# Values a chunk after their unit, denominators a chunk later, K and V in pairs, and another order of the first batch, in an attention layer between two routed feed-forward layers

## What is computed

```python
x = x + 0.5 * ffn(layernorm(x))        # 768 of 1024 tokens, chosen by a router score, go through gelu(x @ w_block)
x = x + attention(layernorm(x))        # 16 heads of 32, causal
x = x + 0.5 * ffn(layernorm(x))
# attention, per batch
q_lat  = einsum('bthd,hdl->bthl', (h @ Wq.T).reshape(b, t, 16, 32), q_to_latent)
logits = einsum('bthl,bsl->bhts', q_lat, h @ Wk_down.T) / sqrt(64)      # latents of 64
attn   = softmax(where(causal, logits, -1e30))
ctx    = einsum('bhts,bsl->bhtl', attn, h @ Wv_down.T)
out    = einsum('bhtl,hld->bthd', ctx, v_up).reshape(b, t, 512) @ Wout.T
```

## Time and profile before

| | us |
|---|---|
| median of 3 runs | 2327.71 (2326.27 to 2329.19) |
| the profiled execution | 2326.99 |
| its span | 2325.1 |
| TensorE busy in it | 2153.9 (93%) |
| VectorE busy | 1760.4 (76%) |
| ScalarE busy | 1101.7 (47%) |
| GpSimd busy | 488.9 (21%) |

### The profile page before, as it was taken

One profiled execution on the slowest core, in us unless ns is written; L12 is line 12 of the kernel. 1 busy time (PEld: TensorE's weight loads), 2 busy tenths in 40 slices (PEclk: granted clock), 3 DMA queues, 4 the chain that ended last, 5 costly groups with the idle time before them and its releaser, 6 DMA issues.

```text
span 2325.1 us, 52505 instructions
## 1 busy us (share of the span) xinstructions
PE 2153.9 (93%) x21256; PEld 1314.2 (57%) x21256; DVE 1760.4 (76%) x5017; ACT 1101.7 (47%) x1942; POOL 488.9 (21%) x574
## 2 busy tenths in 40 slices
PE   5589999999999999999999999999999999999997
PEld 4454477545775456744667446764466544775446
DVE  5668857887678876798677886788857888578747
ACT  2335643456425554255543565435643456435562
POOL 2201212114112231023210232111221113121132
PEclk8789999999999999999999999999999999999999
DMA  4300021210212103021021210211111120212000
GB/s 140 145 1 32 9 73 40 104 42 2 91 55 74 38 14 98 37 74 38 20 91 38 74 39 24 87 44 69 39 58 52 55 93 3 73 37 74 2 2 37
DMA packets 71934, 123.16 MB, mean 53 GB/s; under 512 B 2832, under 2 KB 33040, under 8 KB 67600
## 3 DMA queue, kind: packets, MB, share of 16 engines
q1 hardware_dynamic: 71696, 119.81, 14.8%
HBM read 81.53 MB, written 37.75 MB: 51 GB/s over the span
## 4 chain that ended last, share of the span: by engine, by line
PE 78%; DVE 12%; ACT 5%; issue 4%; POOL 1%; DMA 0%; DVEq 0%; POOLq 0%; SPq 0%; ACTq 0%
PE psum L860 29%; PE psum L873 18%; PE psum L994 11%; PE psum L1001 10%; PE psum L876 5%; DVE part L1143 3%; ACT pr L840 2%; PE psum L887 2%; DVE psum L1145 2%; PE psum L912 2%; DVE junk L1095 1%; DVE junk L1093 1%; DVE qk L1132 1%; PE psum L918 1%; ACT nt_h L746 1%
## 5 line engine op out<-in xcount | busy, mean ns | idle before, releaser
L840 ACT ACTIVATE pr<-psum 128x512 f32<-128x512 f32 x1152 | 617.8, 597 | 525.2 <-PE psum L876 525.0
L873 PE MATMUL psum<-qk,qk 32*128 32x512 f32 (+3 forms) x4608 | 515.3, 370 | 60.6 <-DVE part L1143 22.8
L1145 DVE CUSTOM_DVE_ANT_0 psum<-psum,mask_b 128x512 f32<-128x512 f32 (+3 forms) x1024 | 472.8, 521 | 105.5 <-PE psum L887 103.5
L873 PEld LDWEIGHTS psum<-qk,qk 32*128 32x128 f32 x4608 | 318.5, 186 | 384.0 <-ACT pr L840 337.5
L887 PE MATMUL psum<-qk,qk 32*128 32x512 f32 (+3 forms) x4608 | 511.7, 370 | 20.6 <-DVE part L1143 19.1
L1143 DVE TENSOR_REDUCE part<-psum 128x1 f32<-128x512 f32 x512 | 325.0, 681 | 54.7 <-PE psum L887 52.2
L887 PEld LDWEIGHTS psum<-qk,qk 32*128 32x128 f32 x4608 | 311.0, 186 | 43.0 <-DVE part L1143 22.9
L994 PE MATMUL psum<-pr,v_sb 128*32 128x512 f32 (+3 forms) x3072 | 314.6, 504 | 2.3 <-ACT ht L746 1.6
L1001 PE MATMUL psum<-pr,ones 128*32 128x512 f32 (+3 forms) x3072 | 306.4, 494 | 0.0
L738 POOL TENSOR_SCALAR_AFFINE_SELECT pr<-pr 128x512 f32<-128x512 f32 x256 | 162.0, 654 | 558.4 <-ACT pr L840 556.3
L860 PE MATMUL psum<-wb_h,nt_h 128*128 128x512 f32 x512 | 208.0, 406 | 10.9 <-DVE wb_l L1042 7.0
(11 more groups left out here) (116 smaller groups left out, 3368.0 us busy)
## 6 DMA issues: line engine op xcount, KB each, us to landing
nt_raw<-x_turned_dram SPq DMA_DIRECT2D x16, 1024.0 KB, 6.1
x<-x_dram SPq DMA_DIRECT2D x16, 1024.0 KB, 7.1
spill_x<-x SPq DMA_DIRECT2D x16, 1024.0 KB, 4.7
x<-spill_x SPq DMA_DIRECT2D x16, 1024.0 KB, 6.9
out_dram<-x SPq DMA_DIRECT2D x14, 1024.0 KB, 4.9
w_h<-scratch_o SPq DMA_DIRECT2D x28, 256.0 KB, 3.0
w_l<-scratch_o SPq DMA_DIRECT2D x28, 256.0 KB, 3.3
w_h<-scratch_q SPq DMA_DIRECT2D x6, 1024.0 KB, 4.9
```

Source lines behind the costliest of these rows:

```text
L840: nc.scalar.activation(pr_of(b, g, u)[:, 2 * p + place, :], bank(e, place), ACT.Exp, scale=SCALE).then_inc(exp_ready, 1)
L873: eng.matmul(o, (k_h, k_h, k_l)[t][own, P * j:P * (j + 1)], (q_h, q_l, q_h)[t][own, queries], start=(t == 0 and at == 0), stop=False, skip ...
L1145: m = nc.vector.tensor_tensor_reduce(scores, scores, mask_b[:, BANK - w:BANK], 1.0, FAR, ALU.add, ALU.max, top_of)
```

## The change

`values(n)` (PV and AC) of a unit now stands behind chunk b of the next unit, where it stood behind chunk a of the unit after that. `sums(n)` (DEN and HT) now stands behind chunk a two units later, where it stood behind chunk b. So the two fillings change places and the values come one chunk earlier. At the end of a group what fills the last chunk b is now the values of u7. In group 3 they stand ahead of `F` of tile 1.

Each K is followed by a V in the table, and their six matmuls are issued in turns, K, V, K, V, K, V. TensorE waits for both banks before the first.

In the first batch the statistics of both halves come ahead of the centring and the split of the block weight (`WC`, `WS 0`), all eight router dots come before the first `F`, both broadcasts (`SC`) behind the second `F`, and the splits of the latent and K/V weights before all `RT`. The split of Wq stands inside the second norm's scales, and the split of Wout, now in a buffer of its own, behind the first `Q`. In `closing()` the last `SC` stands behind the layer's tile 5 instead of ahead of it.

```diff
--- before.py
+++ after.py
@@ -123,37 +123,36 @@
     def opening():
 
 
-        out = [("WC", 0)] + sum([raw(0, i) for i in range(TC)], []) + [("WS", 0)]
+        out = sum([raw(0, i) for i in range(TC)], [])
         for c in range(NC):
             for i in range(TC * c, TC * (c + 1)):
                 out += stats(0, 0, i)
             out += scales(0, 0, c)
-        out += sum([raw(0, i) for i in range(TC, NT)], [])
-        for i in range(TC):
+        out += [("WC", 0), ("WS", 0)] + sum([raw(0, i) for i in range(TC, NT)], [])
+        for i in range(NT):
             out += dot(0, 0, i)
-        out += layer(0, 0, 0) + layer(0, 0, 1)
-        for i in range(TC, NT):
-            out += dot(0, 0, i)
-        out += [("SC", 0, 0, 0)] + layer(0, 0, 2) + [("SC", 0, 0, 1)] + [("RT", 0, 0, i) for i in range(3)] + [("WS", 1)]
-        out += [("RT", 0, 0, i) for i in range(3, 6)] + layer(0, 0, 3) + [("WS", 2)] + [("RT", 0, 0, 6), ("RT", 0, 0, 7)]
-        out += [("RF", 0, 0)] + [("GX", 0, 0, i) for i in range(NT)] + [("WS", 3)] + layer(0, 0, 4) + layer(0, 0, 5)
-        out += layer(0, 0, 6) + layer(0, 0, 7)
-        out += summed(0, 0) + summed(0, 1) + summed(0, 2) + summed(0, 3) + scales(1, 0, 0) + [("WS", 4)]
+        out += layer(0, 0, 0) + layer(0, 0, 1) + [("SC", 0, 0, 0), ("SC", 0, 0, 1), ("WS", 1), ("WS", 2)]
+        out += [("RT", 0, 0, i) for i in range(NT)]
+        for i in range(2, NT):
+            out += layer(0, 0, i)
+        out += [("RF", 0, 0)] + [("GX", 0, 0, i) for i in range(NT)]
+        out += summed(0, 0) + summed(0, 1) + summed(0, 2) + summed(0, 3)
+        out += [("VA", 1, 0, 0), ("RS", 1, 0, 0), ("WS", 3), ("NM", 1, 0, 0)]
         out += [("NO", 1, 0, 0), ("NO", 1, 0, 1)]
         after = [summed(0, 4), summed(0, 5), summed(0, 6), summed(0, 7) + scales(1, 0, 1)]
         for i in range(TC):
             out += [("T", 1, 0, i)] + ([("NO", 1, 0, i + 2)] if i + 2 < TC else []) + after[i]
-        out += [("LAT", 0, 0), ("XS", 0, 0), ("NO", 1, 0, 4), ("NO", 1, 0, 5), ("K", 0, 0, 0)]
-        out += [("Q", 0, 0, 0), ("T", 1, 0, 4), ("NO", 1, 0, 6), ("T", 1, 0, 5), ("NO", 1, 0, 7)]
+        out += [("LAT", 0, 0), ("XS", 0, 0), ("NO", 1, 0, 4), ("NO", 1, 0, 5), ("K", 0, 0, 0), ("V", 0, 0)]
+        out += [("Q", 0, 0, 0), ("WS", 4), ("T", 1, 0, 4), ("NO", 1, 0, 6), ("T", 1, 0, 5), ("NO", 1, 0, 7)]
         out += [("Q", 0, 1, 0), ("T", 1, 0, 6), ("T", 1, 0, 7)] + maxima(0, 0, 7) + [("LAT", 0, 1), ("XS", 0, 1)]
-        out += [("XL", 1, 0), ("XL", 1, 1), ("K", 0, 0, 1), ("Q", 0, 0, 1)]
-        beside = [[("Q", 0, 1, 1)], [("K", 0, 1, 0), ("K", 0, 1, 1)], [("V", 0, 0), ("V", 0, 1)], [("Q", 0, 2, 0)],
-                  [("Q", 0, 2, 1)], [("Q", 0, 3, 0)], [("Q", 0, 3, 1)], [("V", 0, 2), ("V", 0, 3), ("V", 0, 4)]]
+        out += [("XL", 1, 0), ("XL", 1, 1), ("K", 0, 0, 1), ("V", 0, 1), ("Q", 0, 0, 1)]
+        beside = [[("Q", 0, 1, 1)], [("K", 0, 1, 0), ("V", 0, 2)], [("K", 0, 1, 1), ("V", 0, 3)], [("Q", 0, 2, 0)],
+                  [("Q", 0, 2, 1)], [("Q", 0, 3, 0)], [("Q", 0, 3, 1)], [("K", 0, 2, 0), ("V", 0, 4), ("K", 0, 2, 1), ("V", 0, 5)]]
         for u, rest in zip((0, 1, 2, 3, 4, 5, 6, 8), beside):
             out += maxima(0, 0, u) + rest + sum([gathered(0, 0, c) for c in range(NC) if LAST[c] == u], [])
             out += turned(0, 0, 1) if u == 8 else []
-        out += [("V", 0, 5), ("V", 0, 6), ("V", 0, 7), ("K", 0, 2, 0), ("K", 0, 2, 1)] + turned(0, 0, 0)
-        return out + [("K", 0, 3, 0), ("K", 0, 3, 1)]
+        out += [("K", 0, 3, 0), ("V", 0, 6)] + turned(0, 0, 0)
+        return out + [("K", 0, 3, 1), ("V", 0, 7)]
...
-        out += [("Q", b, 0, 0), ("Q", b, 1, 0), ("K", b, 0, 0), ("T", 1, b, 4), ("NO", 1, b, 6)]
+        out += [("Q", b, 0, 0), ("Q", b, 1, 0), ("K", b, 0, 0), ("V", b, 0), ("T", 1, b, 4), ("NO", 1, b, 6)]
...
-        out += [("Q", b, 0, 1)] + loads[0] + keys[1] + [("V", b, 0)] + splits[0] + [("V", b, 1)] + splits[1]
+        out += [("Q", b, 0, 1)] + loads[0] + keys[1] + [("V", b, 1)] + splits[0] + splits[1]
...
-            groups[g].append(combined(n, 0) + (then(n - 3, "HR") if n >= 3 else []) + (values(n - 2) if n >= 2 else []))
+            groups[g].append(combined(n, 0) + (then(n - 3, "HR") if n >= 3 else []) + (sums(n - 2) if n >= 2 else []))
             groups[g].append(combined(n, 1) + (then(n - 3, "HE") if n >= 3 else []) + mask(n) + [("MC", *e) for e in closes(n)]
-                             + ([("XT", *e) for e in closes(n - 1)] if n else []) + (sums(n - 2) if n >= 2 else []))
+                             + ([("XT", *e) for e in closes(n - 1)] if n else []) + (values(n - 1) if n >= 1 else []))
         last = len(units) - 1
-        return groups, [then(last - 2, "HR") + then(last - 2, "HE") + values(last - 1), sums(last - 1), values(last),
+        return groups, [then(last - 2, "HR") + then(last - 2, "HE") + sums(last - 1), values(last), [],
                         sums(last) + then(last, "HR") + then(last, "HE")]
...
-        out += dot(1, b, 3) + layer(1, b, 4) + turn(3) + [("SC", 1, b, 0)] + layer(1, b, 5)
+        out += dot(1, b, 3) + layer(1, b, 4) + turn(3) + layer(1, b, 5) + [("SC", 1, b, 0)]
...
+    for e, after in zip(sched, sched[1:]):
+        if e[0] == "K":
+            assert after[0] == "V"
+            beside[e] = after
...
-            raws = [(raw_b, w_block), (raw_lat, w_lat), (raw_kv, None), (raw_o, w_out), (raw_q, w_q)]
+            raws = [(raw_b, w_block), (raw_lat, w_lat), (raw_kv, None), (raw_q, w_q), (raw_o, w_out)]
...
                         sp.wait_ge(split, 8)
-                        eng.dma_start(scratch_o[0], w2_h[:].bitcast(F32)).then_inc(scr_out, 16)
-                        eng.dma_start(scratch_o[1], w2_l[:].bitcast(F32)).then_inc(scr_out, 16)
-                        sp.wait_ge(split, 10)
                         eng.dma_start(scratch_q[0], w2_h[:].bitcast(F32)).then_inc(scr_out, 16)
                         eng.dma_start(scratch_q[1], w2_l[:].bitcast(F32)).then_inc(scr_out, 16)
+                        sp.wait_ge(split, 10)
+                        eng.dma_start(scratch_o[0], wo_h[:].bitcast(F32)).then_inc(scr_out, 16)
+                        eng.dma_start(scratch_o[1], wo_l[:].bitcast(F32)).then_inc(scr_out, 16)
                         sp.wait_ge(scr_out, 64)
...
-                    if n == 4:
-                        act.wait_ge(scr_out, 32)
...
+                    if b == 0 and g >= 2:
+
+                        act.wait_ge(scr_out, 64)
...
-                    pe.wait_ge(split, 10)
+                    pe.wait_ge(split, 8)
...
-                    passes(bank(e), (wkv_h, wkv_l), (lat_h, lat_l), 1, lambda w, n: w[0:L, P * g:P * (g + 1)],
-                           lambda t, n: t[0:L, c * BANK:(c + 1) * BANK]).then_inc(k_done, 1)
-                elif k == "V":
-                    b, i = e[1:]
+                    v = beside[e]
+                    i = v[2]
                     pe.wait_ge(latl_ready, nth["LAT", b, i // TC])
-                    passes(bank(e), (lat_h, lat_l), (wkv_h, wkv_l), 1, lambda t, n: t[L:P, P * i:P * (i + 1)],
-                           lambda w, n: w[L:P, :]).then_inc(v_done, 1)
+                    for user in before[v]:
+                        pe.wait_ge(*freed(*user))
+                    for t, (w, l) in enumerate([(wkv_h, lat_h), (wkv_h, lat_l), (wkv_l, lat_h)]):
+                        m = eng.matmul(bank(e), w[0:L, P * g:P * (g + 1)], l[0:L, c * BANK:(c + 1) * BANK],
+                                       start=(t == 0), stop=(t == 2))
+                        if t == 2:
+                            m.then_inc(k_done, 1)
+                        m = eng.matmul(bank(v), l[L:P, P * i:P * (i + 1)], w[L:P, :], start=(t == 0), stop=(t == 2))
+                        if t == 2:
+                            m.then_inc(v_done, 1)
```

14 lines of the change are left out of this document (9 added, 5 removed).

## The result

The changed kernel takes 2344.16 us (median of 4 runs, 2340.82 to 2348.22) where the kernel before takes 2326.99: ratio 1.0073, interval 1.0057 to 1.0090. It is **slower by 17 us**, outside the range of the prediction and on the other side of the forecast. The profiled execution has a span of 2338.9, 13.8 above the 2325.1 of before.

What follows compares the result with a forecast made beforehand. TensorE, busy 93% of the span, was taken to bound the kernel. Gains of about 30 us against losses of about 26 summed to -4.6, giving 2322.4, or 2323 with 0.7 for the median; range 2308 to 2339.

Steps and rivals of the forecast that it cites:

- 4: Turns of a group: covering TensorE's 0.63 us wait saves 0.55 at 16 turns and 0.5 at 8, -12.8 us.
- 5: End of group 3: values of u7 wait 2.4 us for their mask behind eight GX on POOL, seven times, +16.8 us.
- 6: Step into the latents: one filling less between the last transpositions doubles the 0.41 us wait for VectorE, +2.8 us.
- 7: Granted clock: may drop to half behind the mask wait, less a gain at batch starts, +6.3 us.
- step 1: Opening of batch 0: earlier statistics and ranking, K and V in turns, earlier attention start, -4.8 us.
- 3: First units of a batch: values of u0 fill TensorE's 1.83 us wait for VectorE's maxima, -6.3 us.
- 2: K and V in later batches: issued as pairs, one triple less, 0.7 us in each of 7 batches, -4.9 us.
- 8: End of the last batch: AC of u6 issued a chunk earlier removes a 1.64 us wait for ScalarE, -1.7 us.
- D: K and V: matmuls start strictly in program order, so pairs save two more steps each, -22.5 us, 2301; chance 0.04.
- rival E: Turns of a group: the 0.63 us wait only moves to short fillings in u7 and u8, 2336; chance 0.12.
- rival C: Behind the mask wait: clock drops for 6.6 us at 0.56, 3.3 us lost by each of 7, 2338; chance 0.17.

Runs made afterwards that it cites:

- e1: Changed kernel with the values of u7 in group 3 put back among the next batch's first transpositions: 2307.1 us, ratio 0.9913 to the kernel before.
- e8: Kernel before with the changed opening alone, K and V as before, no swap, old closing: 2325.0 us, ratio 0.9989.
- e4: Kernel before with one part alone, each K issued in turns with a V: 2322.7 us, ratio 0.9985.
- e9: Kernel before with only the values of u0 of batches' first group moved early, behind chunk b of u1: 2338.1 us, ratio 1.0042.
- e6: e1 with the last tile of u5's filling (128 columns) moved to u6: 2301.4 us, ratio 0.9893 to the kernel before.
- e10: Kernel before with 128 columns of u5's fillings moved to u6's, values and denominators where they were: 2319.6 us, ratio 0.9966.
- e2: Changed kernel with the eight GX on POOL behind the mask of u7 in group 3, values still early: 2309.2 us, ratio 0.9920 to the kernel before.
- e7: e1 with the values of u0 of each batch put back late, behind chunk a of u2: 2316.1 us, ratio 0.9954 to the kernel before.
- e5: Kernel before with the swap of values and denominators alone, values of u7 of group 3 staying among the transpositions: 2314.6 us, ratio 0.9952.

## Why the prediction was wrong, step by step

The forecast's sum was -4.6 us; it came out at +13.9 by the profiles (2338.93 against 2325.06) and +17 by the medians. The step that failed by most is 4: the turns of a group were to save 12.8 us and saved some 2, because the waits stayed with the short fillings of u6. With it the size of what follows the wait for the mask was too small (steps 5, 6 and 7: 28.0 forecast, 34.9 measured), and the opening gave 2.1 instead of 4.8.

The table sets the forecast beside the traces, stretch by stretch, as the difference to the kernel before. Its bounds in each batch are the starts of the 1st, 21st, 91st and 121st of the 144 exps (the last two are in the middle of groups 2 and 3), then the start of the next batch's latents and the end of its last K or V. From the 21st exp to the 121st, the kernel after and e1 have done one filling more than the kernel before by the same exp. An estimate of 0.88 us for it (the shortest time of eight such matmuls at full clock) is counted as a gain in the first units and taken off again behind the 121st exp, so the second, fifth and last rows are estimates to that extent.

| stretch | forecast | after | e1 |
|---|---|---|---|
| to the first exp of batch 0 (step 1) | -4.8 | -2.1 | -2.0 |
| first five units of each batch (3, and its clock) | -8.4 | -9.4 | -9.5 |
| 16 turns into groups 1 and 2 (4) | -8.8 | 0.0 | -0.5 |
| 8 turns into group 3 (4) | -4.0 | -2.2 | -2.2 |
| rest of group 3 to the next batch's first latents, 7 times (5, 6, 7) | +28.0 | +34.9 | -0.4 |
| from there to the last K or V, 7 times (2) | -4.9 | -4.7 | -4.5 |
| from there to the next attention | 0 | -1.6 | +1.3 |
| last batch, rest of group 3 to the end (8) | -1.7 | -0.9 | -0.8 |
| sum | -4.6 | +13.9 | -18.6 |

**1. Opening (-4.8 forecast, 2.4 of it K and V).** The way was right as far as the latents. TensorE's first F starts at 27.16 (27.4 said), the ranking at 41.74 (41.6 said), the first latents 3.65 us sooner. The size was not. The first exp of batch 0 is 2.1 us sooner, where the forecast said some 5 for the first scores, and without K and V (e8) it is 0.85.

**2. K and V (-4.9).** The stretch gained 4.7 us in the kernel after, and e4 measured -4.5 in all. Right, and so was the verdict on D.

**3. First units (-6.3, and -2.1 for the clock).** The step said that the values leave the path because they fill the wait. They fill it, but another opens: 1.57 us, ended by VectorE's maxima, since VectorE is the bound there, as the step itself noted. TensorE's idle time in this stretch is 4.7 us *more* than before over the eight batches. What falls is its busy time, with 41 us less at half clock. So the total came out near the forecast (-9.4 against -8.4) by luck: the filled wait, put at 6.3, gave nothing, and the clock, put at 2.1, gave all of it. Alone, the move costs 10 us (e9).

**4. Turns (-12.8).** I covered the wait of 0.63 and put 0.55 down as saved. By the waits, each turn has 0.14 us less (1.04 to 0.90), 3.4 for 24 turns. By the exps it is less still: the lead over the kernel before is 2.75 us ahead of the first turn of batch 1 and 2.6 in the middle of group 1. The 16 turns into groups 1 and 2 gain nothing together, the 8 into group 3 0.27 each. That is the outcome of rival E, to which I gave 0.12. The counterargument was wrong: that ScalarE's exp ends the wait doesn't save it, since a short filling in another place meets the same way over ScalarE to a free bank. E's own reason, that VectorE's maxima set the pace, isn't what the trace shows either; the 0.49 is ended by ScalarE. e6 and e10 show the part of the short fillings from the other side.

**5. Mask (+16.8).** Measured 19.6, seven waits of 2.8 us in the mean, in the range given. The mechanism and its place were right. e1 and e2 show it twice: by moving the values back, and by moving GX on POOL.

**6. Latents (+2.8).** Measured +6.3, 0.9 a batch. The term was mis-sized: I took the wait to double, but VectorE's chain has little slack there, and 0.9 of the 1.33 us of missing filling comes back as a wait.

**7. Clock (+6.3).** Behind the mask 30.7 us were at half clock, where I had 7 x 3.4 x 0.7 = 16.7. In the fifth stretch of the table TensorE is busy 11.5 us longer in the kernel after than in e1, with the same matmuls; that is the cost, where I had 8.4. Three of the six drops lasted 6.8 us, rival C's case, to which I had given 0.17. The answer to C, that TensorE had been busy for 100 us there, misread the rows: its last wait, 0.63 us, was 32 us earlier (546.23 in the kernel before), and in the kernel after 33 us. At the starts of the batches 41 of 44 us of half clock went (seven places of 3.4 to 6.8 us before, one of 3.4 after), for which I had taken off 2.1 us of time.

**8. End (-1.7).** The wait of 1.64 is gone. The kernel after is 15.55 us behind at the last exp and 13.9 at the end. That is -1.7, of which 0.46 is the filling of u6 that the kernel after had done by then. So the stretch gave somewhat less than the size given.

So E came in nearly whole and C by half: 10.6 us less from the turns, 6.9 more behind the mask and at the latents, 2.7 less from the opening. Each of the two rivals stood in the list by itself, and the range ended at 2339 because I left out the case of both. The profiled execution of the kernel after is the fastest of its four; the 3 us between it and the median aren't explained.

How the gain of step 3 divides between levels of clock and waits isn't settled by an experiment of its own: e7 and e9 change the waits as well as the clock, and which of the waits drop the clock was not the same from batch to batch. That the clock is what gives the gain there rests on the busy and idle times of one profile each.

## What to carry to other kernels

When work is moved ahead in a queue, look up who must release it and what is queued ahead of that release on *its* engine: here one mask of 0.6 us behind eight unrelated operations turned a gain of 20 us into a loss of 17, and changing the order on that lightly used engine was enough to get it back. A wait that disappears from its place is not saved until the trace shows that the same releaser does not end a new one a few steps later; count all the waits of the cycle, not the one that is covered. Where an engine's work is moved from one stage to another, ask whether it covered a wait in the stage that it leaves (here the values of u7 did, ahead of the latents: 6.3 us).

## What was not expected of the hardware

- Waits of 2.7 us in TensorE's queue, after 30 us of unbroken work and more, were followed by half clock in six of seven cases, for 3.4 or 6.8 us. One of the same length, 2.71 at 297.94 in batch 0, was not.
- With the values in front of a wait of VectorE at a batch's start and the denominators behind it, the clock stayed at 1.00 in most batches (six of seven in the kernel after, five of seven in e5). With the values alone moved there it fell in all seven (e9). Half clock is 20.4 us in e5 and 54.4 in e9, and 10.7 us lie between their busy times, with the same matmuls; e5 also moves the later fillings.
- K's and V's matmuls, three places apart in the queue, start side by side, at 352.36 and 352.37, so issuing them in turns gained only the triple that had stood alone: -4.5 in e4, not -27. The Trainium skill ("TensorE: Matmul & The Clock Gate", Part 3, "What overlaps and what doesn't") has matmuls start and end strictly in program order; neither the trace nor e4 agrees.
